# Routed stage of a four-layer kernel: where chunk 3's router layers and top-2 search stand in the turn of chunk 2

## The reference, cut to what matters

```python
logits = _gelu(xf @ w_r1 + b_r1) @ w_r2 + b_r2
probs = jax.nn.softmax(logits, axis=-1)
top_p, top_i = jax.lax.top_k(probs, K)            # K = 2 of 8 experts
for _ in range(NUM_ITER):                         # 2 iterations
    ctx = jnp.concatenate([integrated, v], axis=-1)
    # shared network and two chosen experts give alpha, beta, gate;
    # from them x_next and v_next
    halt = jax.nn.sigmoid(_gelu(x_next @ w_h1 + b_h1) @ w_h2 + b_h2)
    refined = _gelu(x_next @ w_f1 + b_f1) @ w_f2 + b_f2
    integrated = integrated + halt * refined * integration_weight
```

## Time and profile before

| | |
|---|---|
| three executions | 846.23, 846.35, 849.56 us |
| the profiled execution | 849.67 us, of which the span from first to last instruction is 847.5 us |
| mean granted TensorE clock | 0.994 of full speed |
| busy share of the span | PE 95%, DVE 75%, ACT 66%, POOL 34% |
| turn (2,0), 471.0 to 502.0 us | PE 29.98 us busy of 31.0 |

### The profile page before, as it was taken

One profiled execution on the slowest core, in us unless ns is written; L12 is line 12 of the kernel. 1 busy time (PEld: TensorE's weight loads), 2 busy tenths in 40 slices (PEclk: granted clock), 3 DMA queues, 4 the chain that ended last, 5 costly groups with the idle time before them and its releaser, 6 DMA issues.

```text
span 847.5 us, 20310 instructions
## 1 busy us (share of the span) xinstructions
PE 808.6 (95%) x7364; PEld 566.2 (67%) x7364; DVE 634.7 (75%) x1587; ACT 563.1 (66%) x1597; POOL 286.8 (34%) x587
## 2 busy tenths in 40 slices
PE   8999999999999999899999999999899989899986
PEld 8887888999998987544444444444566665676652
DVE  5678777777777665766875967765999876899866
ACT  3666667777677776786546586455577779778754
POOL 4255444554444345200000000002157520345445
PEclk9999999999999999999999999999999999999999
DMA  8700000000000000000000000000000000000000
GB/s 338 168 2 1 1 1 2 2 2 1 1 2 2 2 1 2 1 1 0 1 1 0 1 1 0 1 0 1 1 29 3 3 3 1 3 3 3 15 13 27
DMA packets 7887, 13.54 MB, mean 16 GB/s; under 512 B 4343, under 2 KB 5101, under 8 KB 7533
## 3 DMA queue, kind: packets, MB, share of 16 engines
q1 hardware_dynamic: 7788, 12.24, 4.5%
HBM read 11.19 MB, written 1.05 MB: 14 GB/s over the span
## 4 chain that ended last, share of the span: by engine, by line
PE 70%; DVE 13%; ACT 8%; issue 4%; POOL 4%; DMA 1%; DVEq 0%; POOLq 0%; SPq 0%; ACTq 0%
PE psum L1561 10%; PE psum L772 6%; PE psum L812 6%; PE psum L840 6%; PE psum L755 5%; PE psum L764 3%; PE psum L1547 3%; ACT arena L910 2%; PE psum L2016 2%; PE psum L1570 2%; PE psum L1986 2%; PE psum L2528 2%; PE psum L2405 2%; DVE arena L2120 2%; PE psum L1588 2%
## 5 line engine op out<-in xcount | busy, mean ns | idle before, releaser
L517 POOL TENSOR_TENSOR ve<-mv,epsv 128x1 f32<-128x1 f32 x176 | 35.7, 203 | 422.7 <-DVE mv L512 422.7
L1561 PE MATMUL psum<-arena,w1f 128*128 128x512 f32 x240 | 109.5, 592 | 0.0
L520 POOL TENSOR_TENSOR rstd<-ve,epsv 128x1 f32<-128x1 f32 x176 | 101.3, 576 | 13.8
L910 ACT ACTIVATE arena<-psum,negmax 128x128 f32<-128x128 f32 x256 | 90.5, 407 | 22.1 <-DVE negmax L1010 22.1
L1561 PEld LDWEIGHTS psum<-arena,w1f 128*128 128x128 f32 x240 | 45.5, 190 | 48.7 <-issue 44.3
L1100 POOL TENSOR_TENSOR arena<-arena,rsum 128x512 f32<-128x512 f32 x64 | 65.7, 1046 | 24.6 <-DVE rsum L1016 24.6
L1010 DVE TENSOR_REDUCE negmax<-psum 128x8 f32<-128x1024 f32 x32 | 39.2, 1225 | 32.9 <-PE psum L812 32.9
L910 ACT ACTIVATION_READ_ACCUMULATOR arena<-psum,negmax 128x1 f32 x256 | 63.2, 247 | 0.0
L755 PE MATMUL psum<-arena,sclA 128*128 128x128 f32 x512 | 62.5, 275 | 0.1
L526 DVE TENSOR_SCALAR yln<-x_tok,mv,rstd 128x128 f32<-128x128 f32 x128 | 56.6, 454 | 7.9 <-POOL rstd L520 7.5
L772 PE MATMUL psum<-arena 128*128 128x512 f32 x128 | 61.5, 599 | 0.9 <-DVE arena L1005 0.6
(11 more groups left out here) (376 smaller groups left out, 1971.5 us busy)
## 6 DMA issues: line engine op xcount, KB each, us to landing
w<-in_w0qk SPq DMA_DIRECT2D x2, 512.0 KB, 4.8
w<-in_w0vo SPq DMA_DIRECT2D x1, 1024.0 KB, 7.6
cT<-in_cT SPq DMA_DIRECT2D x1, 1024.0 KB, 16.1
out<-x_tok SPq DMA_DIRECT2D x4, 256.0 KB, 2.2
rows<-in_rows SPq DMA_DIRECT2D x1, 836.0 KB, 12.5
x_tok<-in_x_tok SPq DMA_DIRECT2D x1, 768.0 KB, 9.7
ctx_tok<-in_ctx_tok SPq DMA_DIRECT2D x1, 768.0 KB, 11.1
wa<-in_wa SPq DMA_DIRECT2D x1, 768.0 KB, 17.5
```

What stands on the lines that cost most here:

```text
L520: pool.tensor_tensor(rstd[:, u, self.i:self.i + 1], ve[:, u, self.i:self.i + 1], epsv[:, 1:2], ALU.pow) \
L910: m = nc.scalar.activation(e0[:, b, g, :], ps(k, P, j * P), ACT.Exp, bias=negmax0[:, b, g:g + 1], accum_out=sum0[:, b, g:g + 1])
L1561: nc.tensor.matmul(ps(k), w1("e2", j * 384 + arg * D, j * 384 + (arg + 1) * D), f1_Hm[:, n, 2 * j + i, :], start=False, stop=False)
```

## The change

In turn (2,0) the table `moves` of `with_late` gets other places for the jobs R and L of chunk 3, and DVE gets a move, where it had none. On PE, R goes behind G of chunk 1, and L behind W. On ACT, R goes behind ha of chunk 1. On DVE, L goes behind G of chunk 1. The string `FILL_BANKS` is not edited. No instruction is added or taken away.

```diff
             if new == (2, 0):
-                moves = {"pe": [(("R", 3, 0, None), ("X", *new, BETA)), (("L", 3, 0, None), ("ha", *of_old, None))], "act": [(("R", 3, 0, None), ("C", *new, BETA))], "dve": []}[engine]
+                moves = {"pe": [(("R", 3, 0, None), ("G", *of_old, None)), (("L", 3, 0, None), ("W", *new, None))], "act": [(("R", 3, 0, None), ("ha", *of_old, None))],
+                         "dve": [(("L", 3, 0, None), ("G", 1, 1, None))]}[engine]
                 for x, after in moves:
                     order.remove(x)
                     order.insert(order.index(after) + 1, x)
```

## The result

The changed kernel takes 856.05 us (median of four executions, 851.98 to 858.88) against 846.54 us; the ratio is 1.0091, 95% interval 1.0069 to 1.0114, so about 7.7 us slower. Its profiled execution took 854.72 us with a span of 852.7 us, 5.2 us more than the span before. Forecast were 852.2 us, a loss of 5.9, in a range to 855.5; the median lies 0.6 us above that range, though 846.35 times the ratio is 854.1.

The account below looks back on a forecast made before the run. PE was taken to bound the kernel, everything up to F hanging on when it starts B with GATE. 4.16 us of wait plus 1.70 of clock, 5.9, added to the 846.35 median gave 852.2 us, range 849.8 to 855.5.

Parts of the forecast that it names:

- The bank: Turn (2,0): bank 4 holds `xo`, so B with GATE waits for Z(0) on DVE, 499.57 not 495.41: +4.16 us.
- The wait for the GELU: Before L(3) on PE: 0.53 us of wait shrinks to about 0.1; order alone brings B with GATE 0.4 us earlier.
- Rival C: Bank free in time, B with GATE 0.4 us earlier, F at 509.7 to 509.9; 846.05 us, chance 0.04.
- The delay on ACT and in K: ACT's R behind ha delays K's tanh from 500.32 to about 501.4; about 1 us, hidden by the new wait.
- The clock: PE's 4.4 us idle before B with GATE drops the granted clock to 0.50 for one fall: +1.7 us.
- rival B: Clock stays low for two stretches, or falls in the gap and again behind it: +7.6 us, 854.0; chance 0.08.
- so it is paid in full: B and X with GATE follow the wait at once, dense and on the path, so all 1.7 us count.
- rival A: The wait before B with GATE costs 4.2 us but the clock stays at 1.00; 850.5 us, chance 0.25.
- The sum: Wait before B with GATE plus one clock fall: 4.16 + 1.70 = 5.9 us, 0.69% of the profiled execution.
- The difference to a median of only three executions: The 5.9 us loss was added to the timed median of 846.35 us, giving 852.2 us.
- The guess about executions with and without falls: Profiled execution's 3.3 us above the median is about two late clock falls of 1.7 each; quick executions have none.

Follow-up runs that it names:

- the gap filled: Changed kernel plus 17 unused 128x128 identity products that PE computes into free bank 0 while waiting for bank 4; ratio 1.0033, median 850.29 us.
- the shorter gap: Changed kernel with its banks, but DVE takes Z(0) behind G and before L(3); ratio 1.0025.
- 2.22 behind filler: Changed kernel plus 8 unused identity products at the head of PE's wait for bank 4, leaving 2.22 us idle; ratio 1.0046.
- the second occasion: The changed kernel measured again, unaltered; ratio 1.0077, median 854.84 us.

## Why the prediction was right, point by point

*The bank.* Right, and the main part. B was forecast 4.16 us later and came 3.99 later; the steps behind it were 494.10, 496.27 and 498.74 for G, L and Z on DVE, measured 493.84, 496.02 and 498.47 in a turn that began 0.19 earlier. Half of the remaining 0.17 is in these steps, the other half in the step from DVE to PE, 0.06 us (499.15 to 499.21) where 0.15 was taken. That this term is the bank and nothing else is shown from both sides: the order without it costs nothing (0.9995), the bank without the order costs 1.0054.

*The wait for the GELU.* Right that it goes and that PE would reach B about 0.4 us sooner if the bank were free: without the bank B stands 0.27 earlier, as about 0.2 of the wait before L is left. Rival C gave 846.05 us for a free bank, that is within 0.5% of before; both kernels with it free stayed there. Its steps came out too: O(3) at 503.09 and F at 509.68 without a wait, where it has 503.2 and 509.7 to 509.9.

*The delay on ACT and in K.* Right: K's tanh was forecast at 501.4 and stands at 501.36 after the change; it is hidden behind the wait, and costs 1.32 us of waiting at O(3) without it, of which nothing reaches F.

*The clock.* That it falls was right, the size was not: "I take one fall, +1.7 us" measured 2.60 (F with the gap filled against F in the changed kernel). The two stretches at 0.87 and 0.54 lose 0.13 of 5 us and 0.46 of 6 us, together 3.4 us of clock time, twice the 1.70 of the earlier trace rows; 0.8 of them fell into idle time, where they cost nothing. So in this execution the clock did what rival B describes, it fell within the gap and stayed low for two such stretches, but not all of it was paid, and "so it is paid in full" failed as well. That 1.7 comes as near as it does is partly luck: the low clock was taken at half its length and its share in the idle time at nothing. In the profile of the shorter gap it was one fall at 1.7. The argument for rival A, that short waits had kept 1.00, is weak: 1.65 us of waiting was enough for a fall in one execution, 2.22 behind filler was not in another. Nor does the fall of the earlier trace rows stand behind a long wait; the longest there is 0.64 us:

```profile
720.89 0.30 PE L639 MATMUL psum<-const,yln 128*128 128x128 f32 x1 [0.64 <-DVE yln L526]
721.65 0.74 PE L2046 MATMUL psum<-lnT,wa 128*128 128x128 f32 x2 [0.46 <-ACT lnT L649]
```

*The sum.* 3.99 + 2.60 = 6.6 us at F, forecast 5.9. The span grew by 5.2 only; the profiled execution of before has two falls of the clock late in the kernel, and the one after has one, 1.7 us less. Beside the earlier trace rows the second of before, and then the one of after:

```profile
812.00:818.00 6.00, 5.35 (x24) 4.21 (x25) 3.97 (x28) 2.36 (x7) 1.98 (x5) 0.72 0.01 3
```

```profile
722.00:727.00 5.00, 3.90 (x18) 3.71 (x18) 1.72 (x4) 3.77 (x6) 0.00 (x0) 0.66 0.00 0
```

Each loses 1.7 us of clock time (0.28 of 6 us, 0.34 of 5 us). Timed, the loss is 7.7 us (interval 5.8 to 9.6) and on the second occasion 6.5 (4.1 to 9.0); both intervals hold 6.6. The difference to a median of only three executions was the weaker part: the same kernel before has medians of 848.2 to 848.5 over 17 to 25 executions, 2 us above the one shown. With that base the forecast would have been 854.2. The guess about executions with and without falls has some support in the four of the changed kernel: their spans of 850.0, 852.7, 855.4 and 856.8 us go with mean clocks of 0.997, 0.994, 0.988 and 0.986.

## What to carry to other kernels

Where banks or buffers are given out by position in a list, moving a job also changes who waits for whom further on: before a move, go through each shifted output and ask who empties the bank's previous user, and when. A transposed block that only has to be added somewhere was harmless here until a bank on the critical path stood behind it; giving its reader a place in idle time cost nothing (0.9994). A wait of TensorE should be priced with the clock behind it, as a range and not as one number, since the executions of one kernel differ in it. A wait that can't be removed may be cheaper with useless matmuls in it. The kernel before already does so in the wait before F of this turn:

```profile
507.42 0.83 PE L268 MATMUL psum<-const 128*128 128x128 f32 x6
```

## What the runs showed of the hardware

The granted clock does not follow the length of one gap alone. In the profiles it fell behind gaps of 4.10, 3.18 and 1.65 us, and held with 2.22 us behind 2.0 us of filler, with 0.22 us left, and late in the kernel before with 1.62. The same program differs from one execution to the next: with the gap of 3.18 us one execution in six, and with that of 1.65 three in ten, have a mean clock of 0.999, too high for any fall; with 4.1 us none of ten has. The fall costs what dense work meets it: 2.6 us and 2.8 for the two long gaps (3.4 us of clock time lost, the rest of it in the idle time), 1.7 for the short one.
